# Attention's order in a fused decoder layer: maxima nine slots ahead, staging four slots sooner, router turns and counts further behind what they read

## What is computed

```python
x = x + ssm(layernorm(x))                    # Mamba-2-like mixer, 64 heads
x = x + attention(layernorm(x), ctx, ctx)    # 32 query heads, 8 key/value heads of 16
x = x + experts(layernorm(x))                # router over 8 experts, top 2 per token
# attention, per head:
scores = einsum('bkgsd,bktd->bkgst', q, k) / sqrt(16)
out = einsum('bkgst,bktd->bkgsd', softmax(scores), v)
# experts: weights = probs / sum(the two chosen probs); out = sum of 2 weighted gated MLPs
```

## Time and profile before

| quantity | value |
|---|---|
| median of 3 runs | 1481.19 us (1478.87 to 1481.88) |
| the profiled execution's own time | 1481.74 us |
| its span, first to last instruction | 1479.9 us |
| mean granted TensorE clock | 0.945 of full |
| PE busy, DVE busy, ACT busy, POOL busy | 1333.3, 870.6, 724.2, 584.9 us |
| first score of batch 0 | 706.38 us |
| last product of batch 7 starts | 999.73 us |

### The profile page before, as it was taken

The page is one execution under the profiler, slowest core; times in us unless marked ns, Lnnn a source line. Parts: engine busy times, 40 slices in busy tenths (PEclk is TensorE's granted clock), DMA queues, the critical chain, the costliest instruction groups (busy, mean ns, idle before and its releaser), DMA issues.

```text
span 1479.9 us, 22910 instructions
## 1 busy us (share of the span) xinstructions
PE 1333.3 (90%) x7672; PEld 734.5 (50%) x7672; DVE 870.6 (59%) x1819; ACT 724.2 (49%) x1390; POOL 584.9 (40%) x859
## 2 busy tenths in 40 slices
PE   6589999999999998998787778884999999999997
PEld 4456666666666665654233333332444444444443
DVE  4887887979797978757887888645111111111111
ACT  2476667767666776662676767652111111111110
POOL 2345564555455456674223345143122222222221
PEclk9899999999999999997899988875999999999999
DMA  9000000000000000000200000002343444344322
GB/s 330 12 8 6 6 7 1 12 1 12 1 11 2 8 6 8 16 1 1 97 33 33 34 33 31 29 31 72 114 128 65 121 129 129 58 129 128 58 44 29
DMA packets 40276, 73.00 MB, mean 49 GB/s; under 512 B 18529, under 2 KB 22881, under 8 KB 39137
## 3 DMA queue, kind: packets, MB, share of 16 engines
q1 hardware_dynamic: 30224, 48.10, 9.3%
q0 software_dynamic: 8736, 20.61, 7.5%
q10 hardware_dynamic: 1200, 2.82, 0.5%
HBM read 148.91 MB, written 19.99 MB: 114 GB/s over the span
## 4 chain that ended last, share of the span: by engine, by line
PE 65%; DVE 19%; issue 5%; DMA 4%; POOL 3%; ACT 3%; SPq 0%; POOLq 0%; ACTq 0%; DVEq 0%
PE work_ps L533 11%; PE gate_ps L1502 9%; PE up_ps L1502 9%; PE down_ps L1488 9%; PE work_ps L605 7%; DVE conv L814 7%; PE work_ps L538 4%; PE work_ps L627 3%; DVE maxes L1204 3%; PE work_ps L1030 2%; PE mturn_ps L538 2%; DVE mix L730 2%; PE decay_ps L1021 2%; PE decay_ps L615 2%; DMA x_sb<-x_dram 2%
## 5 line engine op out<-in xcount | busy, mean ns | idle before, releaser
L533 PE MATMUL work_ps<-xnT,w_in 128*128 128x256 f32 (+1 forms) x1216 | 301.7, 393 | 1.3 <-ACT xnT L639 0.8
L730 POOL TENSOR_TENSOR mix<-decay,cbm 128x512 f32<-128x512 f32 x128 | 183.0, 1431 | 214.4 <-ACT decay L725 177.4
L533 PEld LDWEIGHTS work_ps<-xnT,w_in 128*128 128x128 f32 (+1 forms) x1216 | 220.5, 189 | 64.1 <-issue 33.3
L721 ACT ACTIVATE decay<-decay_ps 128x512 f32<-128x512 f32 x256 | 154.3, 603 | 112.2 <-PE decay_ps L615 109.7
L1590 POOL DMA_INDIRECT out_dram<-y_out,ids x39 | 61.9, 1587 | 336.0 <-DVE row_w L1554 232.3
L1204 DVE TENSOR_REDUCE maxes<-work_ps 128x2 f32<-128x512 f32 x256 | 166.6, 683 | 44.9 <-PE work_ps L1006 44.0
L814 DVE SCALAR_TENSOR_TENSOR conv<-raw,conv_w,conv 128x256 f32<-128x256 f32 x240 | 180.5, 757 | 6.9 <-ACT conv L681 1.1
L1102 ACT ACTIVATE prob<-decay_ps 128x512 f32<-128x512 f32 x256 | 142.7, 607 | 79.9 <-PE decay_ps L1021 79.0
L1569 DVE TENSOR_TENSOR act<-gelu,up_ps 128x512 f32<-128x512 f32 x39 | 26.8, 687 | 253.9 <-PE up_ps L1502 253.9
L725 ACT ACTIVATE decay<-decay 128x512 f32<-128x512 f32 x256 | 164.1, 641 | 4.7 <-PE work_ps L533 3.0
L1502 PE MATMUL gate_ps<-w_e,xgT 128*128 x312 | 142.2, 599 | 2.0 <-ACT xgT L1519 1.6
(11 more groups left out here) (268 smaller groups left out, 1898.9 us busy)
## 6 DMA issues: line engine op xcount, KB each, us to landing
w_e<-c_experts_dram SPq DMA_DIRECT2D x39, 3072.0 KB
normed_tokens<-r_xn SPq DMA_DIRECT2D x17, 256.0 KB, 2.1
out_dram<-x_sb SPq DMA_DIRECT2D x17, 256.0 KB, 2.6
x_sb<-x_dram SPq DMA_DIRECT2D x1, 3584.0 KB, 22.4
w_in<-c_w_inT_dram ACTq DMA_DIRECT2D x1, 2560.0 KB, 12.0
w_in<-c_w_inT_dram SPq DMA_DIRECT2D x1, 2048.0 KB, 8.6
w_out<-c_w_outT_dram SPq DMA_DIRECT2D x1, 2048.0 KB, 13.6
RT<-cum_scratch SPq DMA_DIRECT2D x32, 48.0 KB
```

The source lines that it names most:

```text
L533: m = e.matmul(ps[0:width, at:at + L], w_in[:, k, col:col + width], xnT[b % 2][:, k, :], start=(k == 0), stop=(k == KD - 1))
L721: e.activation(decay[s % 5][:, :], decay_ps[s % 3][:, :], ACT.Relu, scale=-1.0).then_inc(piece_done[stage], 1)
L730: return e.tensor_tensor(four(mix[s % 5]), four(decay[s % 5]), cb, ALU.mult)
```

## The change

All of it lies in slot numbers. No instruction is added or removed.

- `LEAD` becomes 9. Batch 0's maxima keep a lead of 5 (`FIRST_LEAD`), batch 1's go from 5 to 9 in steps, later batches have 9. `SWEEPS` is built with 9.
- Maxima, their folds and products get fractions of a slot, so that whatever stands at the whole slot comes ahead of them.
- `nmax` moves about four slots earlier, `n_turn` and `n_copy` two. For batches from 1 on, `n_turn` comes two slots behind `nmax`, where both were in one slot.
- Staging of keys and queries moves four slots earlier, its statistics (`q_bn`, `q_stats`) six.
- `r_stats` moves one slot earlier (three for batch 6). `r_turn` comes three slots behind `r_xn` and not one; `r_logit` two slots behind `r_copy` and not one.
- `c_count` moves from beside `c_rank` to eight slots behind it (three in group 2), and group 0 starts eight slots later. `place` moves with it.

The rest of the section shows the orders that result. In everything behind `attention_slots`, L numbers of the changed kernel are five higher.

The core of the diff:

```diff
@@ -41,7 +41,8 @@
 PAIRS = [4, 0, 1, 2, 3]
 ITEMS = [(kh, par, t, quad) for kh in range(2) for par in range(2) for t in range(TPB) for quad in range(4)]
 ODD = [(quad + par) % 2 for kh, par, t, quad in ITEMS]
-LEAD = 5
+LEAD = 9
+FIRST_LEAD = 5
 NORMED = [(0, 2, -44), (2, 4, -13), (4, 16, -11)]
 ROUTED = [(3, 0, 8), (5, 8, 12), (6, 12, 14), (7, 14, 16)]
 ROUND = 1.5 * 2.0 ** 23 * P
@@ -215,40 +216,43 @@
         slots.setdefault(s, []).extend(pieces)
 
     n = len(ITEMS)
-    for i in range(-n - LEAD, NB * n + 4):
+    for m in range(-n, (NB - 1) * n):
+        at = m - FIRST_LEAD - (LEAD - FIRST_LEAD) * min(max(m / n, 0), 1)
+        put(at + 0.1, ("max", m // n + 1, m % n))
+        put(at + 1.2, ("max_fold", m // n + 1, m % n))
+    for i in range(NB * n + 4):
         if 0 <= i < NB * n:
             put(i, ("score", i))
-        if -n <= i + LEAD < (NB - 1) * n:
-            put(i, ("max", (i + LEAD) // n + 1, (i + LEAD) % n))
         if 0 <= i - 1 < NB * n:
             put(i, ("exponent", i - 1))
-        if -n <= i - 1 + LEAD < (NB - 1) * n:
-            put(i, ("max_fold", (i - 1 + LEAD) // n + 1, (i - 1 + LEAD) % n))
         if 0 <= i - 3 < NB * n and (i - 3) % 4 == 3:
-            put(i, ("product", i - 3))
+            put(i + 0.3, ("product", i - 3))
 
     for b in range(NB):
         r = n * (b - 2)
         if b:
-            put(r - 12, ("ctx_in", b))
+            put(r - 16, ("ctx_in", b))
         if b and b % 2 == 0:
             for t in range(2 * TPB):
-                put(r + t, ("q_bn", b * TPB + t))
-            put(r + 4, ("q_stats", b // 2))
-            put(r + 5, ("q_newton", b // 2))
+                put(r - 6 + t, ("q_bn", b * TPB + t))
+            put(r - 2, ("q_stats", b // 2))
+            put(r - 1, ("q_newton", b // 2))
         for t in range(TPB):
             if b:
-                put(r + 2 + 2 * t, ("k_hi", b, t), ("k_lo", b, t))
-                put(r + 10 + 4 * t, ("q", b, t))
-                put(r + 11 + 4 * t, ("q_hi", b, t), ("q_lo", b, t), ("q_dup", b, t))
-            put(r + (10 if b else 16) + 2 * t, ("k_turn", b, t))
-            put(r + (10 + 1 if b else 17) + 2 * t, ("k_copy", b, t))
-            put(r + 15 + 5 * t, ("q_turn", b, t, 0))
-            put(r + 17 + 5 * t, ("q_copy_v", b, t, 0), ("q_turn", b, t, 1))
-            put(r + 19 + 5 * t, ("q_copy_s", b, t, 1))
+                put(r - 4 + 2 + 2 * t, ("k_hi", b, t), ("k_lo", b, t))
+                put(r - 4 + 10 + 4 * t, ("q", b, t))
+                put(r - 4 + 11 + 4 * t, ("q_hi", b, t), ("q_lo", b, t), ("q_dup", b, t))
+            put(r + (6 if b else 16) + 2 * t, ("k_turn", b, t))
+            put(r + (7 if b else 17) + 2 * t, ("k_copy", b, t))
+            q = r + (11 if b else 15) + 5 * t
+            put(q, ("q_turn", b, t, 0))
+            put(q + 2, ("q_copy_v", b, t, 0), ("q_turn", b, t, 1))
+            put(q + 4, ("q_copy_s", b, t, 1))
             put(n * (b - 1) + 6 + t, ("v_in", b, t))
-        put(n * (b - 1) + n - LEAD + 1, ("nmax", b), ("n_turn", b))
-        put(n * (b - 1) + n - LEAD + 2, ("n_copy", b), ("n_out", b))
+        at = n * b - (LEAD if b > 1 else FIRST_LEAD + 4 * b) + 1
+        put(at + 0.3, ("nmax", b))
+        put(at + (2 if b else 0.4), ("n_turn", b))
+        put(at + (3 if b else 1.1), ("n_copy", b), ("n_out", b))
         if b == 1:
             put(2, ("first_expert",))
         for g in range(4):
@@ -260,25 +264,26 @@
         put(f + 8, ("attend", b))
         if b == NB - 1:
             continue
-        late = 4 if b == NB - 2 else 0
-        put(f + 12, ("r_stats", b), ("r_newton", b))
+        late = b == NB - 2
+        put(f + (9 if late else 11), ("r_stats", b), ("r_newton", b))
         for t in range(TPB):
-            put(f + 16 + late + 2 * t, ("r_xn", b, t), ("r_store", b, t))
+            put(f + 17 + late + 2 * t, ("r_xn", b, t), ("r_store", b, t))
             put(f + 20 + late, ("out_in", b, t))
-            put(f + 17 + late + 2 * t, ("r_turn", b, t))
-            put(f + 18 + late + 2 * t, ("r_copy", b, t))
-            put(f + 19 + late + 2 * t, ("r_logit", b, t))
-            put(f + 20 + late + 2 * t, ("r_keep", b, t))
-    for g, at in enumerate((4 * n + 20, 7 * n, 7 * n + 27)):
+            put(f + 20 + late + 2 * t, ("r_turn", b, t))
+            put(f + 21 + late + 2 * t, ("r_copy", b, t))
+            put(f + 23 + late + 2 * t, ("r_logit", b, t))
+            put(f + 24 + late + 2 * t, ("r_keep", b, t))
+    for g, at in enumerate((5 * n - 4, 7 * n - 4, 7 * n + 22)):
         put(at, ("c_scale", g), ("c_newton", g))
-        put(at + 3, ("c_rank", g), ("c_count", g))
-        put(at + 5, ("c_logit", g), ("c_exp", g))
-        put(at + 6, ("c_slots", g))
+        put(at + 6, ("c_rank", g))
+        put(at + (9 if g == 2 else 14), ("c_count", g))
+        put(at + (10 if g == 2 else 7), ("c_logit", g), ("c_exp", g))
+        put(at + (11 if g == 2 else 15), ("c_slots", g))
         if g < 2:
-            put(at + 9, ("c_weight", g), ("c_weight_out", g))
+            put(at + 16, ("c_weight", g), ("c_weight_out", g))
     for t in range(12):
         for c in range(2):
-            put(n * 5 + 4 * t if t < 8 else n * 7 + 8 + 4 * (t - 8) + 2 * c, ("place", c, t))
+            put(n * 5 + 14 + 4 * t if t < 8 else n * 7 + 12 + 4 * (t - 8) + 2 * c, ("place", c, t))
     f = n * NB + 9
     put(f, ("attend_v", NB - 1))
     for t in range(TPB):
```

## The result

The changed kernel takes 1502.39 us (median of 4 runs, 1488.55 to 1504.39), the kernel before 1480.84 beside it (4 runs, 1478.87 to 1481.88). The ratio is 1.0124, 95% interval 1.0092 to 1.0156: **slower by about 18 us**, where 13 us faster were forecast. The profiled execution's own time is 1502.67 us, its span 1500.9.

The account below looks back on a forecast made before the run. Attention was taken as bound by a sum of short waits on PE, with PE, DVE and ACT nearly equally loaded. Removing 30.4 us and adding 17.5 gave -12.9, hence 1468 us, range 1456 to 1482.

Parts of the forecast that it names:

- Terms 1 and 2: PE's waits for negated maxima and, at a batch's first score, for two small DMAs shrink: gains 6.3 and 7.5 us.
- Term 3 (`r_xn`, 8.7): PE's turn of router rows no longer waits for their normalization, given three slots and not one: gain 8.7 us.
- Term 4 (count, 3.6): PE's token count no longer waits behind the ranks, except in the untouched tail: gain 3.6 us.
- Term 5 (products behind `r_stats`, half of 8.7): Products wait less for a bank behind a fold, as key copies move away from router statistics: gain 4.3 us.
- Term 1 (the start): Batch 0's first score comes later because four statistics stand ahead of the copy of negated maxima: adds 1.8 us.
- Term 2 (lost overlap, 17.4 taken at half, 8.7): On PE, 83 maxima lose their overlap with scores at about 0.21 us each: adds 8.7 us, bounds 0 and 17.4.
- The prediction's own test: If batch 3's PE busy time rises by 2.9 us and the batch is not under 34.4 us, lost overlap decided.
- Term 3 (`q_bn` at the end of batches 1 and 3, 4.0): Four statistics and their root now occupy DVE between folds ending batches 1 and 3: adds 4.0 us.
- Term 4 (ranks, 3.0): Group 0's ranks hold DVE for 3.92 us, so PE waits for a bank two maxima later: adds 3.0 us.
- The slower one: Rival: PE becomes the bound through displaced maxima, decisive above 0.26 us apiece: +4.4 us, 1486 us; chance 0.11.
- The clock rival: Rival: with fewer waits the clock also recovers in batches 6 and 7, 9 us more: 1460 us; chance 0.20.

Follow-up runs that it names:

- e11: Repeat of e6, timed in the same job as e12: 1469.84 us, 0.9910 of the kernel before.
- e12: Repeat of e3, with lead 9, timed in the same job as e11: 1469.72 us, 0.9912 of the kernel before.
- e6: e3 with the lead of 5 and the old places of `nmax`, `n_turn` and `n_copy`: 1469.35 us, 0.9915 of the kernel before.
- e7: e3 with the router's statistics, turns and products back at their old slots: 1483.89 us, 0.9997 of the kernel before.
- e8: e3 with the four statistics for batches 2 and 3 behind batch 0's first score again, their root later: 1477.68 us, 0.9957 of the kernel before.
- e9: Kernel before with the router's spacing (turn two slots behind `r_xn`) and group 0's counts four slots later; old staging and lead: 1485.06 us, ratio 1.0019.
- e5: Kernel before with only 70 maxima displaced from directly behind their scores, folds moved too: 1493.89 us, ratio 1.0071.
- e1: Changed kernel with the counts at their old spacing, group 0 still four slots later than before: 1488.77 us, 1.0046 of the kernel before.
- e3: Changed kernel with counts at their old spacing and each maximum straight behind its score again: 1473.53 us, 0.9954 of the kernel before.
- e4: Kernel before with only the groups' ranks, counts, weights and places moved as in the change: 1481.10 us, ratio 1.0011.
- e2: Changed kernel with each maximum and its fold straight behind its score again, counts as changed: 1475.24 us, 0.9959 of the kernel before.

## Why the prediction was wrong

It forecast -12.9 us; the ratio says +18. By its own steps:

**Removed.** Terms 1 and 2 (the turn of the maxima 6.3, the DMAs 7.5): the waits went nearly as described, to 3.4 and 1.3 us, and the lead was worth nothing that can be told (e11 against e12). *This step failed, and it is the largest miss, 13.8 us: a wait's length was taken for its price.* Nor was it all the lead's to remove: with lead 5 the two waits are 13.0 us (e6) and 10.6 (e11), where the kernel before has 17.2. While PE waits at the end of a batch, DVE and ACT go on with what is queued, and PE would have met them a little later. The longer wait for `pv` in e12 fits that reading, which is otherwise argued and not shown. Batch 0's own wait for the negation, forecast to stay at 1.95 us, is 3.10: the statistics stand ahead of it. Term 3 (`r_xn`, 8.7): the wait went, and with the earlier staging the router's spacing is worth 6 to 12 us (e7 against e8 and e6); without it, nothing (e9). Term 4 (count, 3.6): the wait went, but see below. Term 5 (products behind `r_stats`, half of 8.7): wrong. The product's wait became the wait of a `pv_turn` for a bank whose fold is behind the same statistics, four times 2.35 us of the 11.6 in all, here in batch 3, DVE first:

```profile
829.95 1.29 DVE L1245 BATCH_NORM_STATS2 r_bn<-x_sb 128x6 f32<-128x512 f32 x2 [0.74 <-POOL x_sb L1397]
...
832.04 1.28 DVE L1209 TENSOR_REDUCE maxes<-work_ps 128x2 f32<-128x512 f32 x2
```

```profile
832.78 1.11 PE L543 MATMUL work_ps<-ident,pv 128*128 128x128 f32 x4 [2.35 <-DVE maxes L1209]
```

**Added.** Term 1 (the start): 8.26 - 6.30 = 2.0 us against 1.8 forecast, right, and without effect on the end that can be told (e8). Term 2 (lost overlap, 17.4 taken at half, 8.7): *this step failed in size.* The count was right, and so was the pace: PE's work grew by the full price in e5. What halving it assumed, that PE has pauses to take up the rest, holds for the order of the kernel before (10.5 us by the ratio, 7.1 by the profile) and not for the changed one: 14 us within a job (e1 to e3), 15.6 to 18.2 at equal clock. The prediction's own test points the same way: batch 3's PE busy time rose by 5.3 us and the batch is not shorter than 34.4. It forecast 2.9 at most, though, and batch 3's clock fell from 1.00 to 0.91, so part of the 5.3 is the clock. The Trainium skill ("TensorE: Matmul & The Clock Gate", section "The mechanism") says that matmuls start and end in the order of the program. The rows agree: the maximum behind the turn of 826.63 starts at 827.18 and not beside its score. Term 3 (`q_bn` at the end of batches 1 and 3, 4.0) was not tried by itself. Term 4 (ranks, 3.0): *this step failed too*, mis-sized and at the wrong place. I looked for a bank of PE and overlooked ACT, where `c_exp` stood one slot behind the ranks. PE stood 5.49 + 3.15 + 1.05 = 9.7 us there; undoing it gave 3.6 to 9.8 us at equal clock and 12 by the ratios. What the term left out is that the same stall costs nothing by itself (e4).

Along one path of runs: -7 us (e3: lead, staging and router), +14 (e3 to e1: the displaced maxima), +12 (e1 to the changed kernel: the counts) = +19, rounded. By the other path, over e2, it is -7, +1 and +24. Both must come out at the +18 that were measured, since they only cut its ratio into pieces; the two splits differ because the parts interact.

**The rivals.** The slower one named the right mechanism, and its condition (0.26 us per displaced maximum) was not reached, at 0.15 to 0.23. The time went its way, and 16 us past its 1486, because the gains it was set against were not there and a second stall joined; so its sign is partly luck. The clock rival is mixed. In batches 6 and 7, which it was about, the late `r_xn` turns went, the clock rose to 0.87 and 0.74, and the two are 5.5 us shorter. In attention as a whole there is more half speed than before, 130 us and not 84, 47 of them in batch 5. The Trainium skill ("TensorE: Matmul & The Clock Gate", section "A second HAM failure mode: psum-queue depth-cycling") says that short idling between groups of matmuls makes the clock go down and up. The stalls of batch 5 do precede falls: 0.55 from 900 to 910 us, 0.50 from 920 on. But from 930 to 940 us PE was busy 10.00 us of 10 at clock 0.50, and no idling of the trace explains that it stayed there. What brings it back was not settled.

## What to carry to other kernels

Ask of every wait what PE would meet if it were not there: DVE and ACT at 221 and 201 us of a 283 us stretch leave little behind a removed pause (e11), and one experiment on two leads tells how much. Moving a piece by a fraction of a slot is no small edit where neighbours share the matrix engine by row halves; count the pairs it splits and charge each the full pace of work; only where the engine has pauses is part of it free (0.15 us a pair in e5, up to 0.23 in the changed kernel). Behind a long vector-engine block, look at every in-order engine for the first instruction that needs its result, and make sure that nothing of the inner loop is queued behind it; the best version here keeps the maximum beside its score, the counts at their old spacing, and moves only staging and router: 0.991 of the kernel before.

## What the runs showed of the hardware

- Executions of one kernel on one chip differ by 14 us with their mean clock (e2: 1470.03 us at 0.948, 1484.48 at 0.930). Between two chips an event's absolute time moved as well (the first score of one kernel at 704.01 and 707.34 us), while the stretch from the mixer's last projection to it stayed at 8.1 us (e6, e11). A single profile can stand 8 us off its kernel's median, as e2's does (1482.99 against 1475.24).
- The granted clock can stay at half, 1.2 GHz, for the 30 us from 920 to 950 with PE busy 28.6 us of them.
- A stall and a heavier load cost more together than apart: the counts' stall costs 1 to 2 us where PE has room (e2 against e3), and 12 where it has none (the changed kernel against e1, of another job).
- A 49-row score and a 48-row maximum on opposite halves of PE's rows start together, and the next pair 0.22 to 0.23 us later (826.10 and 826.32); with a turn between score and maximum that pace is paid once more, 15.0 us of PE's time for 70 such pairs (e5).
